# k's squares, power and product ahead of the fourth piece of the softmax; LayerNorm of tiles 0 and 1 applied in tile 3; tile 3's moments moved from two queues

## The chip, the cores and the metric

The kernel runs on one core of one Trainium2 chip. The metric is the device time of one execution in microseconds (us). The kernel before takes 2818.89 us, the median of 3 runs (2817.97 to 2821.12).

## The reference

The input is 8 sequences of 512 tokens by 256 features, float32. Three blocks follow each other: half of a transformer of two layers added to the input, a linear memory learned step by step (a scan over tokens), and the same transformer again with the same weights. Each layer of the transformer is

```
h = shift_token(x)                      # second half of the features comes from the token before
q, k, v = split(h @ wqkv)               # 8 heads of 64
q = l2norm(q) * qs;  k = l2norm(k) * ksc
q, k = rotary_xpos(q, k)
o = local_attention(q, k, v)            # windows of 128, each looks at itself and the one before
x = x + o @ wo
h = layernorm(shift_token(x)) * lg + lb
a, g = split(h @ w1 + b1);  x = x + (a * gelu(g)) @ w2 + b2
```

## The kernel before

A sequence of 512 tokens (a "batch" b, 0 to 7) is four tiles t of 128 tokens. The transformer runs twice, so there are four layers L and 32 batch-layers, each a call of `sequence(L, b, ...)` on every engine; between the two passes lies the linear memory (`mid_...`). Each engine has its own program, written out by hand in a fixed order; engines meet only in semaphores. `idx(L, b, t)` counts tiles, and `wait_ge(name, at(name, n))` waits until the n-th event of that name. There is no planner: the order of the calls in `sequence` is the order of the work.

Large products are made from a high and a low part of each operand (`split_product`, three matmuls), so ScalarE copies a product or a transpose out of a PSUM bank as the high part and VectorE subtracts that from the bank for the low part.

One tile of attention, on TensorE (`sequence`, L1223): the scores `S` (L1078) of tile t in two halves; matmuls of the down projection `W2` of the batch before as fillers (`fill`, L1219); `A1`, the q, k, v products of the tile ahead (k first); `PT`, the transposes of the softmax (L1094), four pieces of two heads each; `PV` (L1108), four pieces, the product with v; `A0`, the transposes of x two tiles ahead (L1030); `A2`, the transposes of k and q of the tile ahead (L1054); `WO`, the output projection (lines L1018 to L1020 with `oT`). After tile 2 comes `H2T(L, b, 0)` (L1133 to L1139), which transposes the normalised tiles 0 and 1. After tile 3 come `W1` for tiles 0 and 1, then `H2T(L, b, 1)` between the fifth and the sixth piece, and `W1` for tiles 2 and 3.

The softmax of tile t goes through three engines, piece by piece (j = 0 to 3): VectorE `S` (L1550) adds the mask, scales and takes the minimum; ScalarE `S` (L767) takes the exponentials of two heads and their sums; VectorE `R` (L1559) takes the reciprocals; GpSimd `NP` (L607) multiplies. TensorE's `PT j` waits for `pn_done` of piece j, ScalarE's `PT j` (L778) copies the transpose, and TensorE's `PV j` waits for that (`pt_sb`). After `PV` 3 ScalarE's `O` (L785) and VectorE's `O` (L1564) make `oT`, for which `WO` waits.

k and q of the tile ahead: ScalarE squares them (L743, L746) and copies v (L749); VectorE's `A1` sums the squares (L1518), multiplies with the two rotary tables (L1520, L1523) and adds (L1527), k first; GpSimd's `A1` bounds k's sums from below (L589), raises them to the power -1/2 (L591) and multiplies k by the result (L594), then does guard and power for q (L598, L601). TensorE's `A2` waits for k's product (`krot`) and q's sum (`qrot`). All of GpSimd's `A1` comes after the four `NP` of a tile, all of ScalarE's after the four `S`, all of VectorE's after the four `R`.

LayerNorm needs the moments of a token's own first half and of the second half of the token before. `halves` (L1583, L1584) makes the statistics of a tile, and small DMAs move them by one token. SyncE issues these in `move_stats` (L380 to L386) and `move_first_halves` (L363, L365); for tile 3 the two of `move_first_halves` are issued by ScalarE, just before its first `Gelu` (`G`). `LN_moments` joins them, GpSimd's `LN` (L624) takes the power, `LN_apply` (L1611) normalises. For tiles 0 and 1 (half 0) VectorE does all of it inside tile 2: moments between its k and q parts, applications before and after `O`. Its low part of `H2T(L, b, 0)` (L1577) stands in tile 3 between `R` 0 and `S` 3.

In the first pass, batch 4 stores the split w2 to DRAM (`store_w2`), and batch 0 of each layer splits w2 beside its second half of `W1`.

Of the kernel before, what the change touches and what calls it, by code (L numbers as in the profile page):

```python
# [39 lines left out]
P = 128  # L40
# [23 lines left out]
def build(nc, A):  # L64
    ctx = ExitStack()
    with ctx:
# [295 lines left out]
        def move_first_halves(e, t, q):  # L362
            e.dma_start(stt[0:P - 1, t + 1, 12:18], stt[1:P, t, 0:6]).then_inc(q, 16)  # L363
            if t:
                e.dma_start(stt[P - 1:P, t, 12:18], stt[0:1, t, 0:6]).then_inc(q, 16)  # L365
# [10 lines left out]
        def _(e):  # L376
            def move_stats(L, b, t, q):
# [3 lines left out]
                if t < 3:  # L381
                    move_first_halves(e, t, q)
# [131 lines left out]
            def sequence(L, b, last=False):  # L514
# [33 lines left out]
                if L < DEPTH and b == 4:  # L548
                    store_w2(L)
# [29 lines left out]
        def _(e):  # L579
            def A1(L, b, t, LN_of=None):  # L580
# [14 lines left out]
                if LN_of:  # L595
                    LN(*LN_of)
# [39 lines left out]
            def sequence(L, b, prev, nxt):  # L636
                for t in range(NT):
# [3 lines left out]
                    for j in range(4):  # L641
                        NP(L, b, t, j)
                    if ahead:
                        A1(*ahead, (L, b, 0) if t == 2 else None)
# [9 lines left out]
            def transformer(ps):  # L654

                A1(DEPTH * ps, 0, 0)
# [75 lines left out]
        def _(e):  # L732
# [6 lines left out]
            def A1(L, b, t):  # L739
# [3 lines left out]
                e.activation(sq[:, 0, :], bank[0][:, :], ACT.Square).then_inc(sqk, 1)  # L743
                e.wait_ge(q_ps, at(q_ps, m + 1))
# [103 lines left out]
            def sequence(L, b, prev, nxt):  # L848
                for t in range(NT):
                    ahead = (L, b, t + 1) if t < NT - 1 else nxt and (*nxt, 0)  # L850
                    ahead2 = (L, b, t + 2) if t < NT - 2 else nxt and (*nxt, t - 2)
                    for j in range(4):
                        S(L, b, t, j)
                    if ahead:
                        A1(*ahead)
                    for j in range(4):
                        PT(L, b, t, j)
                    O(L, b, t)
                    if ahead2:
                        A0(*ahead2)  # L860
                    if ahead:
                        A2(*ahead)
                    if t == 2:
                        H2T(L, b, 0)
# [4 lines left out]
                move_first_halves(e, 3, st_moved[1])  # L869
# [6 lines left out]
                for mt in range(MT):  # L876
                    G(L, b, 1, mt)
                    U_hi(L, b, MT + mt - 1)
                    if L < DEPTH and b == 0 and 1 <= mt <= 3:
                        split_w2_hi(L, mt - 1)  # L880
# [9 lines left out]
            def transformer(ps):  # L890
# [7 lines left out]
                A1(DEPTH * ps, 0, 0)  # L898
# [116 lines left out]
        def _(e):  # L1015
# [66 lines left out]
            def PT(L, b, t, j):  # L1082
# [7 lines left out]
                if j == 0 and t in (0, 3):  # L1090
                    e.wait_ge(h2t_lo, at(h2t_lo, 2 * b + 16 * L + (t == 3)))
# [35 lines left out]
            def H2T(L, b, half):  # L1127

                done = 9 * b + (72 * L + 4 * half)
                e.wait_ge(pt_sb, at(pt_sb, 4 * idx(L, b, 2 + half) + 4))  # L1130
# [92 lines left out]
            def sequence(L, b, prev, nxt):  # L1223
                for t in range(NT):
# [22 lines left out]
                    PV(L, b, t, 0)  # L1247
                    PT(L, b, t, 3)
                    for j in range(1, 4):
                        PV(L, b, t, j)  # L1250
# [8 lines left out]
                    if t == 2:  # L1259
                        H2T(L, b, 0)  # L1260
# [231 lines left out]
        def _(e):  # L1492
# [5 lines left out]
            def A1(L, b, t, LN_of=None):  # L1498
# [14 lines left out]
                for i, (squared, rotated, added, sums, summed, read) in enumerate((  # L1513
                        (sqk, rotk, kr_step, ssk, ssk_done, guard_k), (sqq, rotq, qrot, ssq, ssq_done, guard_q))):
                    f = 2 * (1 - i)
                    e.wait_ge(squared, at(squared, m + 1))
                    e.wait_ge(read, at(read, m))
                    e.tensor_reduce(sums[:, :], sq[:, i, :].rearrange("p (h d) -> p h d", h=HEADS), AX.X, ALU.add).then_inc(summed, 1)  # L1518
# [9 lines left out]
                    if LN_of and i == 0:  # L1528
                        LN_moments(*LN_of)
# [181 lines left out]
            def sequence(L, b, prev, nxt):  # L1711
                for t in range(NT):
# [6 lines left out]
                    if t == 3:  # L1719
                        H2T(L, b, 0)  # L1720
                    S(L, b, t, 3)
                    for j in range(1, 4):
                        R(L, b, t, j)
                        if L == 0 and b < B - 1 and j < 3:
# [6 lines left out]
                    if ahead:  # L1731
                        A1(*ahead, (L, b, 0) if t == 2 else None)
                    if L == 0 and b < B - 1 and t == 0:
                        entry_stats(b + 1, 3)
                    if t == 2:
                        LN_apply(L, b, 0, 0, 3)
                    O(L, b, t)
                    if ahead2:
                        A0(*ahead2)
# [302 lines left out]
```

## Time and profile before

| | |
|---|---|
| median of 3 runs | 2818.89 us |
| profiled execution, its own time | 2823.89 us |
| its span, first to last instruction | 2822.1 us |
| mean granted TensorE clock | 0.988 of 2.4 GHz |
| busy share: PE, DVE, ACT, POOL | 95%, 76%, 62%, 56% |
| the chain that ended last: PE, DVE, ACT, issue, POOL | 52%, 19%, 12%, 8%, 7% |

PE is TensorE's matmuls, DVE VectorE, ACT ScalarE, POOL GpSimd. L12 is line 12 of the kernel; a line can be that of a helper, so L1018 to L1020 are the matmuls of every split product, told apart by the tiles they read. The ends of matmuls are modelled, so starts are the surer times; times on POOL are rough. Everything below comes from this one execution.

### The profile page before, as it was taken

The numbers are of one execution on the slowest core, as the hardware profiler recorded it, in microseconds if no ns is written. First come the engines' busy times: TensorE is split into PE (matmuls) and PEld (weight loads), VectorE is DVE, ScalarE is ACT, GpSimd is POOL, SyncE is SP. The second block draws the span as 40 slices with busy tenths as digits, with TensorE's granted clock in tenths as the row PEclk, the third lists the DMA queues.
The fourth block names the chain that finished last, engine by engine and source line by source line (L and its number), as shares of the span: only waits on it lengthen the run. The fifth ranks groups of instructions, "written<-read, shape, count | busy, mean of one in ns | idle before, by whom it ended". The sixth has DMA issues, their size and how long they took to land.

```text
span 2822.1 us, 66713 instructions
## 1 busy us (share of the span) xinstructions
PE 2690.0 (95%) x23280; PEld 2319.4 (82%) x23280; DVE 2146.8 (76%) x6398; ACT 1757.2 (62%) x4748; POOL 1577.9 (56%) x1758
## 2 busy tenths in 40 slices
PE   7999999999999999998999999999999999999998
PEld 6888888888888888887776788888888888888887
DVE  7788888877777877776655887777777778877875
ACT  4666666666666665665454666666666666666664
POOL 4565666556555665654212566655556566656554
PEclk8999999999999999999999999999999999999999
DMA  3121011002000000004100000000003000000000
GB/s 113 31 76 58 24 51 53 20 24 104 13 2 2 2 2 24 2 2 163 58 17 31 2 2 2 2 2 2 2 2 109 32 2 17 17 17 17 17 16 24
DMA packets 75899, 81.33 MB, mean 29 GB/s; under 512 B 37552, under 2 KB 61872, under 8 KB 74416
## 3 DMA queue, kind: packets, MB, share of 16 engines
q1 hardware_dynamic: 69792, 75.51, 8.1%
q8 instruction: 189, 3.10, 0.5%
q10 hardware_dynamic: 5776, 1.56, 0.2%
q14 instruction: 142, 1.16, 0.1%
HBM read 49.53 MB, written 26.74 MB: 27 GB/s over the span
## 4 chain that ended last, share of the span: by engine, by line
PE 52%; DVE 19%; ACT 12%; issue 8%; POOL 7%; ACTq 2%; DMA 1%; DVEq 0%; POOLq 0%
PE bank L1018 9%; PE bank L1020 8%; PE bank L1019 8%; ACT pr L767 7%; PE bank L1219 5%; PE bank L1108 4%; PE bank L1078 4%; PE bank L1094 3%; PE bank L1054 3%; DVE t L1523 3%; DVE t L1520 3%; PE bank L1363 2%; POOL pr L607 2%; DVE pr L1550 2%; DVE h L1611 2%
## 5 line engine op out<-in xcount | busy, mean ns | idle before, releaser
L607 POOL TENSOR_TENSOR pr<-pr,rden 128x512 f32<-128x512 f32 (+1 forms) x512 | 467.6, 940 | 516.6 <-DVE rden L1559 512.7
L767 ACT ACTIVATE pr<-pr,nb 128x256 f32<-128x256 f32 (+1 forms) x1024 | 479.5, 470 | 276.5 <-DVE nb L1550 273.4
L1550 DVE CUSTOM_DVE_ANT_0 pr<-bank,maskb,r 128x256 f32<-128x256 f32 (+1 forms) x1024 | 401.8, 447 | 26.8 <-PE bank L1078 17.6
L1018 PE MATMUL bank<-h2T,w 128*128 128x256 f32 x1408 | 406.8, 289 | 12.9 <-DVE h2T L1577 12.9
L1019 PE MATMUL bank<-h2T,w 128*128 128x256 f32 x1408 | 395.9, 281 | 0.0
L1020 PE MATMUL bank<-h2T,w 128*128 128x256 f32 x1408 | 395.7, 281 | 0.0
L634 POOL TENSOR_TENSOR uTl<-t,uTh 128x256 fp32r<-128x256 f32 x320 | 238.1, 748 | 277.3 <-ACT uTh L842 277.3
L1625 DVE SCALAR_TENSOR_TENSOR t<-bank,b,t 128x256 f32<-128x256 f32 (+1 forms) x384 | 181.8, 480 | 215.5 <-ACT t L830 102.2
L1018 PE MATMUL bank<-wqkv,hT 128*128 128x512 f32 x768 | 306.2, 399 | 8.5 <-DVE nb L1550 5.7
L1019 PE MATMUL bank<-wqkv,hT 128*128 128x512 f32 x768 | 305.5, 398 | 0.0
L1020 PE MATMUL bank<-wqkv,hT 128*128 128x512 f32 x768 | 302.5, 394 | 0.0
L778 ACT ACTIVATE pT<-bank 128x512 f32<-128x512 f32 (+1 forms) x512 | 250.9, 550 | 68.0 <-PE bank L1094 67.9
L1018 PEld LDWEIGHTS bank<-h2T,w 128*128 128x128 f32 x1408 | 268.0, 190 | 22.9 <-DVE h2T L1577 19.0
L1019 PEld LDWEIGHTS bank<-h2T,w 128*128 128x128 f32 x1408 | 270.7, 192 | 0.0
L1108 PE MATMUL bank<-pT,v 128*64 128x128 f32 x3584 | 263.9, 283 | 6.2 <-ACT pT L778 1.9
L1020 PEld LDWEIGHTS bank<-h2T,w 128*128 128x128 f32 x1408 | 265.7, 189 | 0.0
L1094 PE MATMUL bank<-ident,pr 128*128 128x128 f32 x1792 | 249.1, 279 | 6.2 <-POOL pr L607 6.2
L1108 PEld LDWEIGHTS bank<-pT,v 128*64 128x64 f32 x3584 | 201.2, 137 | 55.8 <-issue 51.9
L827 ACT ACTIVATE t<-bank,b 128x256 f32<-128x256 f32 x320 | 151.5, 474 | 149.6 <-PE bank L1020 145.2
L1094 PEld LDWEIGHTS bank<-ident,pr 128*128 128x128 f32 x1792 | 202.9, 142 | 47.4 <-issue 22.4
L1219 PE MATMUL bank<-w2h,uTh 128*128 128x256 f32 (+1 forms) x768 | 237.7, 310 | 2.9 <-issue 1.5
L1078 PE MATMUL bank<-kT,qT 64*128 64x256 f32 (+1 forms) x3072 | 232.9, 286 | 3.8 <-issue 2.9
(229 smaller groups left out, 6978.3 us busy)
## 6 DMA issues: line engine op xcount, KB each, us to landing
wqkv<-wqkv_split SPq DMA_DIRECT2D x18, 512.0 KB, 6.2
w<-w_split SPq DMA_DIRECT2D x3, 2816.0 KB, 9.9
Y<-in_x SPq DMA_DIRECT2D x8, 512.0 KB, 8.2
out<-Y SPq DMA_DIRECT2D x8, 512.0 KB, 3.5
stt<-stt SPq DMA_DIRECT2D x224, 3.0 KB
h<-out SPq DMA_DIRECT2D x7, 512.0 KB, 3.9
out<-h SPq DMA_DIRECT2D x7, 512.0 KB, 2.9
wqkv_split<-wqkv SPq DMA_DIRECT2D x1, 3072.0 KB, 11.7
```

Source lines behind the costliest of these rows:

```text
L607: e.tensor_tensor(pr[:, 2 * j:2 * j + 2, 0:wide], pr[:, 2 * j:2 * j + 2, 0:wide], rden[:, 2 * j:2 * j + 2].unsqueeze(2).to_broadcast([P, 2 ...
L634: e.tensor_tensor(uTl[:, half, JOBS[i], :], ut[:, job % 2, :], uTh[:, half, JOBS[i], :], ALU.subtract).then_inc(u_lo, 1)
L767: last = e.activation(pr[:, hd, 0:wide], pr[:, hd, 0:wide], ACT.Exp, bias=nb[:, hd:hd + 1], scale=-1.0, accum_out=den[:, hd:hd + 1])
L778: e.activation(pT[:, 2 * j:2 * j + 2, 0:w, :], bank[PT_BANK[j]][:, :].rearrange("p (h w c) -> p h w c", h=2, w=2)[:, :, 0:w, :], ACT.Copy) ...
L1018: e.matmul(out, left[0], right[0], start=first, stop=False)
L1019: e.matmul(out, left[0], right[1], start=False, stop=False)
L1020: return e.matmul(out, left[1], right[0], start=False, stop=last)
L1078: m = e.matmul(out, qT[rows, lq, p, :], kT[rows, lk, p, slots, :], start=(i == 0), stop=(i == 2), skip_group_check=True)
L1094: mm = e.transpose(bank[bk][:, (2 * g + w) * P:(2 * g + w + 1) * P], pr[:, 2 * j + g, w * P:(w + 1) * P], ident[:, :])
L1108: mm = e.matmul(bank[6][64 * g:64 * g + 64, j * P:(j + 1) * P], v[:, tile, hd * DH:(hd + 1) * DH], pT[:, hd, w, :], start=(w == 0), stop=( ...
L1219: mm = e.matmul(bank[bk][:, 0:D], left, right, start=(unit == 0), stop=(unit == UNITS - 1))
L1550: m = e.tensor_tensor_reduce(pr[:, hd, 0:wide], bank[j][:, g * 256:g * 256 + wide], far, r[:, t, 1, place(hd):place(hd) + 1], FAR, ALU.add ...
```

## The change

In each tile that has a tile ahead, three engines do k's part earlier. ScalarE squares k before its fourth pair of exponentials; VectorE sums k's squares before its fourth reciprocal (`squares` is the old code as a function); GpSimd does guard, power and product of k before the fourth `NP`. On TensorE `PV` 1 and 2 go ahead of `PT` 3. LayerNorm's moments of tiles 0 and 1 are joined after the second reciprocal of tile 2, GpSimd's `LN` goes behind q's power, and the four applications go between the reciprocals of tile 3; `H2T(L, b, 0)` goes behind `PV` 3 of tile 3 on all three engines. Of tile 3's three statistics moves SyncE issues two and ScalarE one row only (before: SyncE one, ScalarE two). `U_rest` goes ahead of `LN_moments` in the first half of `W1`. `store_w2` waits for the statistics to have moved, and w2 is split one piece of `W1` earlier.

```diff
-        def move_first_halves(e, t, q):
-            e.dma_start(stt[0:P - 1, t + 1, 12:18], stt[1:P, t, 0:6]).then_inc(q, 16)
-            if t:
-                e.dma_start(stt[P - 1:P, t, 12:18], stt[0:1, t, 0:6]).then_inc(q, 16)
+        def move_first_row(e, t, q):
+            e.dma_start(stt[P - 1:P, t, 12:18], stt[0:1, t, 0:6]).then_inc(q, 16)
...
                 e.wait_ge(st_done, at(st_done, idx(L, b, t) + 1))
                 e.dma_start(stt[1:P, t, 6:12], stt[0:P - 1, t + 1, 18:24]).then_inc(q, 16)
-                if t < 3:
-                    move_first_halves(e, t, q)
+                e.dma_start(stt[0:P - 1, t + 1, 12:18], stt[1:P, t, 0:6]).then_inc(q, 16)
+                if 0 < t < 3:
+                    move_first_row(e, t, q)
...
                 if L < DEPTH and b == 4:
+                    stats_moved(L, b)
                     store_w2(L)
...
@@ -638,10 +640,15 @@
                     ahead = (L, b, t + 1) if t < NT - 1 else nxt and (*nxt, 0)
                     if prev:
                         XB(*prev, t)
-                    for j in range(4):
+                    for j in range(3):
                         NP(L, b, t, j)
                     if ahead:
-                        A1(*ahead, (L, b, 0) if t == 2 else None)
+                        A1_k(*ahead)
+                    NP(L, b, t, 3)
+                    if ahead:
+                        A1_q(*ahead)
+                    if t == 2:
+                        LN(L, b, 0)
...
                 for t in range(NT):
                     ahead = (L, b, t + 1) if t < NT - 1 else nxt and (*nxt, 0)
                     ahead2 = (L, b, t + 2) if t < NT - 2 else nxt and (*nxt, t - 2)
-                    for j in range(4):
+                    for j in range(3):
                         S(L, b, t, j)
                     if ahead:
-                        A1(*ahead)
+                        A1_k(*ahead)
+                    S(L, b, t, 3)
+                    if ahead:
+                        A1_qv(*ahead)
                     for j in range(4):
                         PT(L, b, t, j)
                     O(L, b, t)
+                    if t == 3:
+                        H2T(L, b, 0)
                     if ahead2:
                         A0(*ahead2)
                     if ahead:
                         A2(*ahead)
-                    if t == 2:
-                        H2T(L, b, 0)
                 for i in next_pieces(L, b)[0:1]:
                     next_hi(i)
                 table(ACT.Gelu)
                 e.wait_ge(st_done, at(st_done, idx(L, b, 3) + 1))
-                move_first_halves(e, 3, st_moved[1])
+                move_first_row(e, 3, st_moved[1])
...
                 for mt in range(MT):
                     G(L, b, 1, mt)
                     U_hi(L, b, MT + mt - 1)
-                    if L < DEPTH and b == 0 and 1 <= mt <= 3:
-                        split_w2_hi(L, mt - 1)
+                    if L < DEPTH and b == 0 and mt < 3:
+                        split_w2_hi(L, mt)
...
@@ -1087,8 +1102,8 @@
                     e.wait_ge(nb_done, at(nb_done, 4 * n + 4))
                 else:
                     e.wait_ge(pt_sb, at(pt_sb, 4 * n + (0, -2, 0, 1)[j]))
-                if j == 0 and t in (0, 3):
-                    e.wait_ge(h2t_lo, at(h2t_lo, 2 * b + 16 * L + (t == 3)))
+                if j == 0 and t == 0:
+                    e.wait_ge(h2t_lo, at(h2t_lo, 2 * b + 16 * L))
...
-                e.wait_ge(pt_sb, at(pt_sb, 4 * idx(L, b, 2 + half) + 4))
+                e.wait_ge(pt_sb, at(pt_sb, 4 * idx(L, b, 3) + 4))
...
                     PT(L, b, t, 1)
                     PT(L, b, t, 2)
                     fill(1)
-                    PV(L, b, t, 0)
+                    for j in range(3):
+                        PV(L, b, t, j)
                     PT(L, b, t, 3)
-                    for j in range(1, 4):
-                        PV(L, b, t, j)
+                    PV(L, b, t, 3)
+                    if t == 3:
+                        H2T(L, b, 0)
                     if ahead2:
                         A0(*ahead2)
                     if ahead:
@@ -1256,8 +1273,6 @@
                     if ahead:
                         A2(*ahead, 1)
                     WO(L, b, t)
-                    if t == 2:
-                        H2T(L, b, 0)
                     fill(3)
...
+                for i, (rotated, added) in enumerate(((rotk, kr_step), (rotq, qrot))):
                     f = 2 * (1 - i)
-                    e.wait_ge(squared, at(squared, m + 1))
-                    e.wait_ge(read, at(read, m))
-                    e.tensor_reduce(sums[:, :], sq[:, i, :].rearrange("p (h d) -> p h d", h=HEADS), AX.X, ALU.add).then_inc(summed, 1)
+                    if i:
+                        squares(m, 1)
...
-                    if LN_of and i == 0:
-                        LN_moments(*LN_of)
+
+            def squares(m, i):
+
+                squared, sums, summed, read = ((sqk, ssk, ssk_done, guard_k), (sqq, ssq, ssq_done, guard_q))[i]
+                e.wait_ge(squared, at(squared, m + 1))
+                e.wait_ge(read, at(read, m))
+                e.tensor_reduce(sums[:, :], sq[:, i, :].rearrange("p (h d) -> p h d", h=HEADS), AX.X, ALU.add).then_inc(summed, 1)
...
                     S(L, b, t, 1)
                     S(L, b, t, 2)
                     R(L, b, t, 0)
-                    if t == 3:
-                        H2T(L, b, 0)
                     S(L, b, t, 3)
                     for j in range(1, 4):
+                        if j == 3 and ahead:
+                            squares(idx(*ahead), 0)
                         R(L, b, t, j)
+                        if t == 2 and j == 1:
+                            LN_moments(L, b, 0)
+                        if t == 3 and j < 3:
+                            LN_apply(L, b, 0, 2 * j - 2, 2 * j)
                         if L == 0 and b < B - 1 and j < 3:
...
                     if ahead:
-                        A1(*ahead, (L, b, 0) if t == 2 else None)
+                        A1(*ahead)
                     if L == 0 and b < B - 1 and t == 0:
                         entry_stats(b + 1, 3)
-                    if t == 2:
-                        LN_apply(L, b, 0, 0, 3)
                     O(L, b, t)
+                    if t == 3:
+                        H2T(L, b, 0)
                     if ahead2:
                         A0(*ahead2)
-                    if t == 2:
-                        LN_apply(L, b, 0, 3)
                     if ahead:
                         A2(*ahead)
                     WO(L, b, t)
...
                 for mt in range(MT):
                     U(L, b, 0, mt)
                     if mt == 1:
+                        U_rest(L, b, 0)
                         LN_moments(L, b, 1)
-                        U_rest(L, b, 0)
                     if mt == 2:
...
@@ -1762,8 +1782,8 @@
                     U(L, b, 1, mt)
                     if mt == 1:
                         U_rest(L, b, 1)
-                    if L < DEPTH and b == 0 and mt > 2:
-                        split_w2_lo(L, mt - 3)
+                    if L < DEPTH and b == 0 and 2 <= mt <= 4:
+                        split_w2_lo(L, mt - 2)
```

## Rows read from the trace of the kernel before

**Rows 1.** The page, part 1: busy us (share of the span) xinstructions.

```profile
PE 2690.0 (95%) x23280; PEld 2319.4 (82%) x23280; DVE 2146.8 (76%) x6398; ACT 1757.2 (62%) x4748; POOL 1577.9 (56%) x1758
```

**Rows 2.** Who TensorE waited for, whole run: us in total, times, longest.

```profile
PE bank L1018 <- DVE oT L1564: 32.4, 40, 1.0
...
PE bank L1135 <- DVE h L1611: 11.8, 25, 3.8
```

**Rows 3.** Timeline of GpSimd, tile 1: start, us, operation, count, [idle before <-releaser].

```profile
2271.43 4.04 POOL L607 TENSOR_TENSOR pr<-pr,rden 128x512 f32<-128x512 f32 x4 [5.01 <-DVE rden L1559]
2275.43 0.24 POOL L589 TENSOR_SCALAR ssg<-ssk 128x8 f32<-128x8 f32 x1
2275.76 1.66 POOL L591 TENSOR_TENSOR r<-ssg,small 128x8 f32<-128x8 f32 x1
2277.57 1.04 POOL L594 TENSOR_TENSOR t<-t,r 128x512 f32<-128x512 f32 x1
```

**Rows 4.** Timeline of ScalarE, tile 1.

```profile
2272.65 0.49 ACT L767 ACTIVATE pr<-pr,nb 128x256 f32<-128x256 f32 x1
...
2273.64 0.58 ACT L743 ACTIVATE sq<-bank 128x512 f32<-128x512 f32 x1
...
2277.52 0.60 ACT L778 ACTIVATE pT<-bank 128x512 f32<-128x512 f32 x1 [0.46 <-PE bank L1094]
```

**Rows 5.** Timeline of VectorE, tile 1.

```profile
2273.77 0.17 DVE L1559 RECIPROCAL rden<-den 128x2 f32<-128x2 f32 x1 [0.82 <-ACT pr L767]
...
2274.25 0.69 DVE L1518 TENSOR_REDUCE ssk<-sq 128x8 f32<-128x512 f32 x1 [0.31 <-ACT sq L743]
```

**Rows 6.** Timeline of TensorE, tile 1.

```profile
2276.23 0.66 PE L1108 MATMUL bank<-pT,v 128*64 128x128 f32 x8
2276.82 0.66 PE L1094 MATMUL bank<-ident,pr 128*128 128x128 f32 x4
2277.41 1.58 PE L1108 MATMUL bank<-pT,v 128*64 128x128 f32 x24
2278.92 0.44 PE L1030 MATMUL bank<-ident,Y 128*128 128x128 f32 x2
...
2280.50 0.36 PE L1018 MATMUL bank<-wo,oT 128*128 128x256 f32 x1
```

**Rows 7.** Timeline of GpSimd, tile 0.

```profile
2260.59 0.24 POOL L589 TENSOR_SCALAR ssg<-ssk 128x8 f32<-128x8 f32 x1 [0.56 <-DVE ssk L1518]
```

**Rows 8.** Timeline of TensorE, tile 0.

```profile
2263.34 0.44 PE L1030 MATMUL bank<-ident,Y 128*128 128x128 f32 x2
...
2265.69 0.36 PE L1018 MATMUL bank<-wo,oT 128*128 128x256 f32 x1
```

**Rows 9.** Timeline of TensorE, tile 2.

```profile
2293.72 0.44 PE L1030 MATMUL bank<-ident,Y 128*128 128x128 f32 x2
...
2296.31 0.36 PE L1018 MATMUL bank<-wo,oT 128*128 128x256 f32 x1 [0.88 <-DVE oT L1564]
```

**Rows 10.** Timeline of GpSimd, tile 3.

```profile
2302.60 1.04 POOL L607 TENSOR_TENSOR pr<-pr,rden 128x512 f32<-128x512 f32 x1 [5.26 <-DVE rden L1559]
2304.13 3.04 POOL L607 TENSOR_TENSOR pr<-pr,rden 128x512 f32<-128x512 f32 x3 [0.49 <-DVE rden L1559]
```

**Rows 11.** Timeline of TensorE, tile 3.

```profile
2309.88 0.44 PE L1030 MATMUL bank<-ident,Y 128*128 128x128 f32 x2
```

**Rows 12.** Stretches: length and busy us (x) of PE, PEld, DVE, ACT, POOL; PEclk; DMA.

```profile
756.00:759.30 3.30, 1.90 (x21) 1.58 (x19) 3.30 (x9) 2.61 (x6) 1.46 (x2) 1.00 0.00 0
759.40:766.20 6.80, 6.80 (x29) 5.80 (x29) 2.40 (x17) 3.87 (x17) 3.76 (x6) 0.50 0.01 2
2295.40:2298.80 3.40, 2.52 (x23) 2.39 (x23) 3.36 (x9) 0.83 (x3) 1.94 (x2) 1.00 0.00 0
745.10:828.00 82.90, 79.49 (x636) 69.51 (x636) 63.52 (x187) 52.71 (x144) 47.24 (x53) 0.96 0.02 5
828.00:907.20 79.20, 76.77 (x636) 66.99 (x636) 60.78 (x184) 50.98 (x141) 47.20 (x53) 1.00 0.01 2
```

More of the change, by code:

```diff
@@ L579, in _, with A1_k @@
         def _(e):
-            def A1(L, b, t, LN_of=None):
+            def A1_k(L, b, t):
                 m = idx(L, b, t)
@@ L594, in A1, with A1_q @@
                 e.tensor_tensor(heads(kr), heads(kr), r[:, t, 0, :].unsqueeze(2).to_broadcast([P, HEADS, DH]), ALU.mult).then_inc(krot, 1)
-                if LN_of:
-                    LN(*LN_of)
+            def A1_q(L, b, t):
+                m = idx(L, b, t)
+                minus_half = small[:, 0:1].to_broadcast([P, HEADS])
                 e.wait_ge(ssq_done, at(ssq_done, m + 1))
@@ L654, in transformer @@
             def transformer(ps):
-                A1(DEPTH * ps, 0, 0)
+                A1_k(DEPTH * ps, 0, 0)
+                A1_q(DEPTH * ps, 0, 0)
                 if ps == 0:
@@ L737, in A0, with A1_k @@
                 e.activation(columns(hT, 0, t * P, P), cut(bank[2][:, 0:D], KT), ACT.Copy).then_inc(ht_hi, 1)
-            def A1(L, b, t):
+            def A1_k(L, b, t):
                 m = idx(L, b, t)
@@ L743, in A1, with A1_qv @@
                 e.activation(sq[:, 0, :], bank[0][:, :], ACT.Square).then_inc(sqk, 1)
+            def A1_qv(L, b, t):
+                m = idx(L, b, t)
                 e.wait_ge(q_ps, at(q_ps, m + 1))
@@ L897, in transformer @@
                     split_hi(2)
-                A1(DEPTH * ps, 0, 0)
+                A1_k(DEPTH * ps, 0, 0)
+                A1_qv(DEPTH * ps, 0, 0)
                 A0(DEPTH * ps, 0, 1)
@@ L1496, in A0, with A1 @@
                 e.tensor_tensor(columns(hT, 1, t * P, P), cut(bank[2][:, 0:D], KT), columns(hT, 0, t * P, P), ALU.subtract).then_inc(ht_lo, 1)
-            def A1(L, b, t, LN_of=None):
+            def A1(L, b, t):
                 m = idx(L, b, t)
@@ L1511, in heads @@
                     return ap.rearrange("p (h c j) -> p h c j", h=HEADS, c=2)
-                for i, (squared, rotated, added, sums, summed, read) in enumerate((
-                        (sqk, rotk, kr_step, ssk, ssk_done, guard_k), (sqq, rotq, qrot, ssq, ssq_done, guard_q))):
+                for i, (rotated, added) in enumerate(((rotk, kr_step), (rotq, qrot))):
                     f = 2 * (1 - i)
-                    e.wait_ge(squared, at(squared, m + 1))
-                    e.wait_ge(read, at(read, m))
-                    e.tensor_reduce(sums[:, :], sq[:, i, :].rearrange("p (h d) -> p h d", h=HEADS), AX.X, ALU.add).then_inc(summed, 1)
+                    if i:
+                        squares(m, 1)
                     e.wait_ge((kt_ps, qt_ps)[i], at((kt_ps, qt_ps)[i], m))
@@ L1803, in transformer @@
                     e.tensor_copy(maskb[:, :, :, :].rearrange("p a w k -> p (a w k)"), mask_raw)
+                squares(idx(DEPTH * ps, 0, 0), 0)
                 A1(DEPTH * ps, 0, 0)
```

## The prediction

> **What bounds the kernel now.** I read the page's first part, then who waited for whom on TensorE, then one batch in order of time, engine by engine, and last the granted clock. The first part says that TensorE is busy 95% of the span [rows 1]: whatever the other engines do counts only where TensorE stands still. The table of waits says where: 32.4 us in the output projection for VectorE's `oT`, 11.8 us in front of the transposes of tiles 2 and 3 for LayerNorm's `h` [rows 2]. So the present waits are worth a few tens of us in 2819, and the question is what new ones the change makes. I work it on batch 1 of the last layer (its tiles lie between 2254 and 2314 us), whose pattern repeats in 32 batch-layers of about 79 us.
>
> **The moved k part on GpSimd, tile 1.** In time order GpSimd normalises four pieces of the softmax (`NP`) one after the other, 4.04 us from 2271.43, and only then does k's guard, power and product: 2275.43, 2275.76, 2277.57 to 2278.61, so 3.14 us from the first start to when the next can start [rows 3]. The change puts these 3.14 us ahead of piece 3. Are k's sums there in time? ScalarE squares k now at 2273.64, after the fourth pair of exponentials; that pair starts at 2272.65 [rows 4], so the new Square starts there and the pair behind it (its input is k's product, the first of three that TensorE makes meanwhile). VectorE's reduce follows a Square by 0.61 (2274.25 after 2273.64) and takes 0.69 [rows 4, 5]: done at 2273.95, before GpSimd has finished piece 2 at 2274.46. The fourth pair's exponentials slip by 0.48 us, VectorE's last reciprocal from 2273.77 to 2274.25, and the rotation of k still starts a little earlier than now; its sum is ready before the power ends. So nothing holds the k part up, and nothing shortens it: piece 3 ends at 2274.46 + 3.14 + 1.04 = 2278.6 instead of 2275.5.
>
> **What TensorE does about it.** It transposes piece 3 (`PT 3`) now at 2276.82, 1.3 us after the piece is ready; PV 1 to 3 start at 2277.41 and the next step, A0, at 2278.92 [rows 6]. The new order puts PV 1 and 2 ahead of PT 3. PV 0 with its change-over takes 0.59, three more take 1.51, so PV 0 to 2 are over at 2276.23 + 0.59 + 1.01 = 2277.8. Piece 3 comes at 2278.7 with a semaphore's delay: TensorE stands 0.9 us. Then the second price of the new order: ScalarE's copy of PT 3 starts 0.70 after it (2277.52 after 2276.82) and takes 0.60 [rows 4, 6]; with 0.1 for the release PV 3 starts 1.4 after PT 3. Before, PV 1 and 2 lay in between; now nothing does, and 0.6 of the 1.4 is PT 3 itself: another 0.8. A0 starts at 2278.7 + 1.4 + 0.5 = 2280.6, 1.7 us late. Behind PV 3 everything follows PV 3: the copy and difference of `oT` set the output projection (`WO`) 1.58 us after A0 [rows 6], as now. Tile 1 costs **+1.7 us**. The first wait is bounded by 0 (GpSimd not late at all) and 1.9 (TensorE profits nothing from PV 1 and 2), the second by 0 and 1.4.
>
> **Tile 0.** Its pieces are half as wide. The power cannot start before the sums, and k's guard now starts at 2260.59, after a wait for them [rows 7]; with the Square one pair earlier I take 0.9 less, so the k part runs 2259.7 to 2262.8 and piece 3 to 2263.4. The same two waits put A0 1.5 late. But between A0 and WO there are now 2.35 us instead of tile 1's 1.58 [rows 8], waits for k's and q's rotation, and these 0.8 vanish, since VectorE is ahead. **+0.7** (bounds -0.8 and 1.7).
>
> **Tile 2.** A0 at 1.7 late as in tile 1. WO comes 2.59 after A0 because VectorE still has the moments and four applications of LayerNorm to do before `oT`; TensorE waits 0.88 for it there [rows 9]. The change takes both away (moments to the wait for exponentials after the second reciprocal, applications to tile 3), so WO is 1.58 after A0 again: 1.7 - 1.0 = **+0.7** (bounds -1.0 and 1.7). The moments need tile 1's moved statistics some 4.6 us earlier than now; if these are late, the wait falls first on VectorE's own wait for exponentials, so I take 0 (bounds 0 and 0.5 a batch). GpSimd's `rs` now stands behind q's power, where it is idle.
>
> **Tile 3.** Now VectorE puts `h2T` between reciprocal 0 and the fourth pair, and GpSimd starts piece 1 only at 2304.13 [rows 10]. With `h2T` gone pieces 0 to 2 run from 2302.60 to 2305.7; four applications lie between the reciprocals, 0.3 us each, where VectorE waited for exponentials. Piece 3 ends at 2305.7 + 3.14 + 1.04 = 2309.8; PT 3 would be reached at 2308.6. Wait 1.2, then 0.8. A0 now is at 2309.88 [rows 11]; it comes 1.9 late. One wait behind it (0.2, k's product) goes; but H2T (0.7 us of TensorE) leaves tile 2, where it lay between WO and the scores, and VectorE is not ready for the scores that much sooner: 0.2 back. **+1.9**, in 30 of 32 cases, since after the last batch of each pass no tile is ahead. H2T itself only moves, and ScalarE's and VectorE's copies of it lie under A0, A2, WO and the last fill before W1 needs them.
>
> **The rest.** Tile 3's moments: SyncE now issues two of the moves and ScalarE one, so gelu starts up to 0.7 us earlier and LayerNorm's second half some tenths earlier. That recovers at most the 11.8 us of waits for `h`, among them one of 3.8 which falls where `store_w2` is issued, which now stands behind a wait [rows 2]; I take 11 (bounds 0 and 12). w2's split one step earlier: the batch that has it takes 82.9 us instead of 79.2 [rows 12], twice in the run: 7.4 (bounds 0 and 7.4). Both together give **-18**.
>
> The Trainium skill, page "DMA: Bandwidth & Descriptors", section "Issuing engines are not separate DMA queues", says that DMAs of several engines run on the same 16 DMA engines, and that starting them from two saves only the sequencer's time. By that rule alone the ordinary `h` waits (8 of my 11 us) would stay, and the sum would be 3010. I go by the row, since ScalarE's issue time is what gelu waits behind.
>
> **The clock.** In the stretch 756.0 to 759.3, with a stall in it, TensorE was busy 1.90 of 3.30 us at full clock, and from 759.4 to 766.2 it was granted 0.50, which is 1.2 GHz; around tile 2's present stall, 2295.4 to 2298.8, it was busy 2.52 of 3.40 and kept 2.4 GHz [rows 12]. The new stages have about 1.7 us (tiles 1 and 2) or 2.0 us (tile 3) of stall within 3 us, so they are like the first stretch or worse, and how they fall varies from stage to stage. Most of the 3.7 us by which that batch is longer is stall 1.4 and clock 2.3. I take one fall in four stages (a third of tiles 1 and 2, half of tile 3, few of tile 0: 35 falls) at 1.3 us, as part of a fall lies under waits: **+45** (bounds 0 and 128 falls of 2.3, 294).
>
> **Sum.** 32 x (0.7 + 1.7 + 0.7) = 99, and 30 x 1.9 = 57: 156. Less 18, plus 45: +183. The profiled execution took 2823.89 us for a span of 2822.1, 5 us above the median 2818.89; the differences are taken from it and put on the median: **3002 us**.
>
> **Rivals.**
> *The clock stays up.* The stalls come as worked out, but full clock is kept, as through today's 0.88: 2819 + 156 - 18 = 2957. For it: the stalls lie between transposes and products, never one long gap. Against: 756.0. Chance 0.22.
> *The clock falls in most stages.* 96 falls at 1.5: 2957 + 144 = 3101. Chance 0.15.
> *Only the second wait.* If piece 3 is there by the end of PV 2, tile 1 costs 0.8, tile 0 -0.2, tile 2 -0.2, tile 3 +0.8: 32 x 0.4 + 30 x 0.8 - 18 = +19, 2838. It needs 0.9 us less on GpSimd; spans on it are rough, but that is more than a quarter of the k part [rows 3]. Chance 0.03.
> *The other side, faster.* The place is PT 3. If GpSimd's k part took under 1.5 us instead of 3.14, piece 3 and its copy would lie wholly under PV 1 and 2, and the stalls of today would be the whole effect: 32.4 and 11.8 [rows 2], 0.8 in 32 tiles 0 [rows 8], 7.4 [rows 12], together 77: 2742. Nothing in the trace shows a power of less than 1.6 us. Chance 0.04. That it lands within 0.2%: 0.02.
>
> **How the numbers follow.** My case has 0.54; its own range is 2960 to 3050. The range for 8 in 10 leaves the faster cases and the extreme clock out: 2915 to 3085. A measurement of this kernel tells 0.2% (6 us) from no change; faster 0.04, same 0.02, slower 0.94.
>
> **What would show it.** In the trace after: TensorE waits in PT (L1094's form) for GpSimd's product with `rden` some 0.9 us in each tile, 126 times, and in PV for ScalarE's copy of pT as often, 0.8 us; the wait of WO for `oT` in tile 2 is gone; H2T follows PV 3 of tile 3; the wait for `h` is near nothing; a batch takes 84 us or more; the clock shows 0.5 in many short stretches, all behind PT 3. Wrong it is if piece 3's product does not start after k's, if TensorE reaches PT 3 later than 2 us after PV 0, or if the granted clock stays near 0.99.

## The result: 9.8% slower, and the profile after

| | before | after |
|---|---|---|
| median | 2818.43 us (2816.38 to 2821.12) | 3093.81 us (3089.06 to 3103.08) |
| ratio | | 1.098, 95% interval 1.0951 to 1.101 |
| profiled execution: time, span | 2823.89, 2822.1 us | 3097.28, 3095.5 us |
| mean granted TensorE clock | 0.988 | 0.958 |
| stretches granted 0.5, in all | 12, 68.0 us | 55, 263.7 us |

Slower, as forecast, but by 275 us and not by 183. The page's first part, the chain that ended last, and who TensorE waited for (us in total, times, longest):

```profile
PE 2761.2 (89%) x23280; PEld 2396.3 (77%) x23280; DVE 2254.7 (73%) x6398; ACT 1752.1 (57%) x4748; POOL 1592.7 (51%) x1758
...
PE 43%; POOL 21%; DVE 16%; issue 11%; ACT 8%; DMA 0%; DVEq 0%; ACTq 0%; SPq 0%; POOLq 0%
```

```profile
PE bank L1109 <- POOL pr L609: 182.8, 130, 2.7
PE bank L1123 <- ACT pT L789: 82.4, 132, 0.7
...
PE bank L1150 <- DVE h L1629: 2.9, 8, 1.2
```

TensorE's share falls from 95% to 89% [rows 1], and GpSimd has 21% of the chain where it had 7%. L1109 is `PT`, L1123 `PV`, L1150 the first transpose of `h`. The wait for `oT` (32.4 us in 40 places, rows 2) is gone from the head of the table, that for `h` at the first transpose fell from 11.8 to 2.9, and two waits stand in nearly every tile that were next to nothing. Tile 1 of a batch, GpSimd and then TensorE, answers to rows 3 and 6:

```profile
2843.89 3.04 POOL L609 TENSOR_TENSOR pr<-pr,rden 128x512 f32<-128x512 f32 x3 [5.55 <-DVE rden L1577]
2846.90 0.24 POOL L589 TENSOR_SCALAR ssg<-ssk 128x8 f32<-128x8 f32 x1
2847.22 1.67 POOL L591 TENSOR_TENSOR r<-ssg,small 128x8 f32<-128x8 f32 x1
2849.03 1.04 POOL L594 TENSOR_TENSOR t<-t,r 128x512 f32<-128x512 f32 x1
2850.03 1.04 POOL L609 TENSOR_TENSOR pr<-pr,rden 128x512 f32<-128x512 f32 x1
```

```profile
2848.69 1.55 PE L1123 MATMUL bank<-pT,v 128*64 128x128 f32 x24
2851.13 0.66 PE L1109 MATMUL bank<-ident,pr 128*128 128x128 f32 x4 [0.89 <-POOL pr L609]
2852.47 0.67 PE L1123 MATMUL bank<-pT,v 128*64 128x128 f32 x8 [0.69 <-ACT pT L789]
2853.07 0.44 PE L1045 MATMUL bank<-ident,Y 128*128 128x128 f32 x2
```

Piece 3 starts 3.13 us after the guard starts (3.14 worked out), TensorE waits 0.89 for it (0.9) and 0.69 for the copy (0.8). From VectorE's first score of tile 1 to that of tile 2 it is 16.50 us, where before it was 14.81: +1.69 against +1.7. The same distance of tile 0 went from 14.39 to 15.03: +0.64 against +0.7.

Tile 3 is where it parts. VectorE, GpSimd and TensorE there, in this order:

```profile
2792.38 0.16 DVE L1577 RECIPROCAL rden<-den 128x2 f32<-128x2 f32 x1
2792.45 0.35 DVE L1624 TENSOR_TENSOR lead<-mv,rs 128x2 f32<-128x2 f32 x1
2792.73 1.40 DVE L1629 TENSOR_SCALAR h<-Y,mv,rs 128x128 f32<-128x128 f32 x2
2794.05 0.15 DVE L1577 RECIPROCAL rden<-den 128x2 f32<-128x2 f32 x1
2794.12 1.30 DVE L1629 TENSOR_SCALAR h<-Y,mv,rs 128x128 f32<-128x128 f32 x2
2795.35 0.67 DVE L1547 TENSOR_REDUCE ssk<-sq 128x8 f32<-128x512 f32 x1
```

```profile
2791.75 2.04 POOL L609 TENSOR_TENSOR pr<-pr,rden 128x512 f32<-128x512 f32 x2 [5.26 <-DVE rden L1577]
2794.28 1.06 POOL L609 TENSOR_TENSOR pr<-pr,rden 128x512 f32<-128x512 f32 x1 [0.49 <-DVE rden L1577]
2796.11 0.24 POOL L589 TENSOR_SCALAR ssg<-ssk 128x8 f32<-128x8 f32 x1 [0.77 <-DVE ssk L1547]
```

```profile
2800.33 0.66 PE L1109 MATMUL bank<-ident,pr 128*128 128x128 f32 x4 [2.58 <-POOL pr L609]
2801.67 0.67 PE L1123 MATMUL bank<-pT,v 128*64 128x128 f32 x8 [0.69 <-ACT pT L789]
```

Two applications that I put at 0.3 us each take 1.40 and 1.30 together. Each pair ends only after GpSimd's product beside it has: 2794.13 against 2793.79, 2795.42 against 2795.34. In all 32 batches one of the two takes 1.14 us in the first pair and 1.06 in the second, and the other 0.32 to 0.34. Reciprocal 2 and the sum of k's squares come later for it, so GpSimd stands 0.49 and 0.77, and TensorE waits 2.58 where I had 1.2. In tile 2 the same is seen on a smaller scale, with LayerNorm's moments in their new place (`vare` is the variance, made by a `TENSOR_SCALAR` too); VectorE, then TensorE:

```profile
2776.17 0.92 DVE L1617 TENSOR_SCALAR vare<-mv 128x4 f32<-128x4 f32 x1
2777.01 0.15 DVE L1577 RECIPROCAL rden<-den 128x2 f32<-128x2 f32 x1
```

```profile
2782.48 0.66 PE L1109 MATMUL bank<-ident,pr 128*128 128x128 f32 x4 [1.10 <-POOL pr L609]
```

The Trainium skill, page "SBUF — State Buffer", section "Who interferes with whom", says that VectorE and GpSimd share a pair of ports as an exclusive lock, that `tensor_scalar` is among VectorE's operations that can take the pair, and that whoever issues first holds it for the whole instruction. The trace agrees: `h` is made by `TENSOR_SCALAR`, and its pair is stretched from 0.6 to 1.40 us beside a product of 1.04 us. The application that was already running when the product began kept its 0.32. That it is the ports which VectorE waits for is the page's account; the runs below show only that these instructions are slow beside GpSimd's products and others are not.

Two whole batches of after, one without a stretch of low clock and one with three (length; busy us of PE, PEld, DVE, ACT, POOL; PEclk; DMA):

```profile
2716.90:2802.30 85.40, 76.41 (x638) 66.91 (x636) 66.35 (x187) 50.53 (x140) 47.90 (x53) 1.00 0.05 14
2450.80:2540.20 89.40, 80.39 (x638) 70.60 (x636) 64.35 (x183) 50.84 (x140) 48.07 (x53) 0.94 0.08 25
```

At full clock a batch is 6.2 us longer than the 79.2 of rows 12: 32 x 6.2 = 198 us. The rest, about 77 of the 275, goes with the clock. Of the 55 stretches at 0.5, 23 begin in tile 3, 15 in tile 2, 5 in tile 1 and 7 in tile 0, most of them behind `PT` 3; before there were 2, 1, 0 and 3.

### The profile page after: what moved, and what is told of

Read it like the earlier page. It is cut to its first block, busy times and chain, and to the rows that moved or that the text cites. A ratio compares the mean times of both kernels' runs of the same rounds, so it can differ in the third digit from the quotient of the medians.

```text
span 3095.5 us, 66726 instructions
## 1 busy us (share of the span) xinstructions
PE 2761.2 (89%) x23280; PEld 2396.3 (77%) x23280; DVE 2254.7 (73%) x6398; ACT 1752.1 (57%) x4748; POOL 1592.7 (51%) x1758
## 4 chain that ended last, share of the span: by engine, by line
PE 43%; POOL 21%; DVE 16%; issue 11%; ACT 8%; DMA 0%; DVEq 0%; ACTq 0%; SPq 0%; POOLq 0%
POOL pr L609 10%; PE bank L1033 6%; PE bank L1035 6%; PE bank L1034 5%; POOL r L591 5%; PE bank L1069 5%; PE bank L1234 5%; DVE pr L1568 4%; PE bank L1123 3%; PE bank L1109 3%; DVE h L1629 2%; ACT pT L789 2%; ACT pr L778 2%; PE bank L1378 2%; PE bank L1045 2%
## 5 line engine op out<-in xcount | busy, mean ns | idle before, releaser
L1109 PE MATMUL bank<-ident,pr 128*128 128x128 f32 x1792 | 255.2, 283 | 182.9 <-POOL pr L609 182.8
L1109 PEld LDWEIGHTS bank<-ident,pr 128*128 128x128 f32 x1792 | 206.2, 144 | 233.3 <-POOL pr L609 215.5
L1123 PE MATMUL bank<-pT,v 128*64 128x128 f32 x3584 | 270.6, 292 | 84.0 <-ACT pT L789 82.4
L1123 PEld LDWEIGHTS bank<-pT,v 128*64 128x64 f32 x3584 | 204.7, 141 | 142.0 <-ACT pT L789 114.3
L1582 DVE TENSOR_TENSOR oT<-bank,oT 128x512 fp32r<-128x512 f32 x128 | 88.5, 692 | 281.0 <-ACT oT L796 281.0
L626 POOL TENSOR_TENSOR rs<-vare,small 128x4 f32<-128x4 f32 x64 | 69.7, 1088 | 342.4 <-DVE vare L1617 342.4
```

The lines of the kernel that those rows point to most:

```text
L1109: mm = e.transpose(bank[bk][:, (2 * g + w) * P:(2 * g + w + 1) * P], pr[:, 2 * j + g, w * P:(w + 1) * P], ident[:, :])
L1123: mm = e.matmul(bank[6][64 * g:64 * g + 64, j * P:(j + 1) * P], v[:, tile, hd * DH:(hd + 1) * DH], pT[:, hd, w, :], start=(w == 0), stop=( ...
```

## The experiments

The changes below are against the kernel after, unless they say before. "Kernel 3" is the kernel of experiment 3, and so on; of two kernels under one number it is the first. The runs of before that stood beside them had medians of 2817 to 2822 us.

**1. The parts alone.** Three kernels from the kernel before, each with one part of the diff shown ahead: the k part with TensorE's order; LayerNorm's place (with `H2T`); the rest (moments, `store_w2`, w2's split).

> The k part of the change alone (ScalarE's Square, VectorE's sums, GpSimd's guard, power and product ahead of the fourth piece; PV 1 and 2 ahead of PT 3); LayerNorm, the statistics moves and w2's split as before. Theory A (two new waits on TensorE in every tile, 1.7 us in tile 1): most of the 275 us comes from here, 2819 + 155 for the waits + 40 to 80 for the granted clock, 3010 to 3055. Rival B (LayerNorm's applications in tile 3, which took 1.40 and 1.30 us for two instead of 0.6 in the trace after, are what my sum missed and the greater part): under 2960.

> LayerNorm's part alone (moments after the second reciprocal of tile 2, applications between the reciprocals of tile 3, H2T behind PV 3 of tile 3). Theory A: it takes 1.0 us of WO's wait out of tile 2 and puts up to 1.5 us of VectorE into tile 3, of which the transposes of k wait for about 1: 2800 to 2840. Rival B: 2870 or more.

> The rest alone (tile 3's moves from two queues, U_rest ahead of the moments, store_w2 behind a wait, w2 split one step earlier). As predicted -18: 2801; if the two-queue move brings nothing and only the two single stalls go, -8 to -11: 2809.

| part | median, us | ratio, 95% interval | against before |
|---|---|---|---|
| k part | 3034.95 | 1.0754 (1.0729 to 1.0779) | +213 |
| LayerNorm | 2797.16 | 0.9921 (0.9907 to 0.9936) | -24 |
| the rest | 2809.72 | 0.9961 (0.9946 to 0.9976) | -12 |
| sum of the three | | | +177 |
| all together | 3093.81 | 1.098 (1.0951 to 1.101) | +275 |

The k part came out as expected (3010 to 3055), the rest as in its second case (2809), and the LayerNorm part 3 us below its range. The two other parts are gains by themselves, and together with the k part they cost 98 us more than the sum. Some of that was never to be had: with the k part alone the wait for `oT` is nearly gone already (before 32.4), since `PV` 3 comes later there, and LayerNorm's new place can't take it away a second time:

```profile
PE bank L1033 <- DVE oT L1584: 3.1, 6, 1.0
```
In the LayerNorm part the applications are as slow as in the change:

```profile
2282.81 1.40 DVE L1609 TENSOR_SCALAR h<-Y,mv,rs 128x128 f32<-128x128 f32 x2
2284.20 1.30 DVE L1609 TENSOR_SCALAR h<-Y,mv,rs 128x128 f32<-128x128 f32 x2
```

There they cost TensorE nothing at `PT` 3 (it waits 6.1 us there in all, before 6.2), since piece 3 has slack. With the k part ahead of piece 3 that slack is spent. In the rest alone, the wait for `h` went from 11.8 us to

```profile
PE bank L1135 <- DVE h L1611: 5.8, 27, 1.2
```

so the one wait of 3.8 is gone and the ordinary ones mostly stay; that is 6 of the 11 us I had counted. The Trainium skill, page "DMA: Bandwidth & Descriptors", section "Issuing engines are not separate DMA queues", says that issuing from several engines saves only the issuing time on the sequencer, by which I had the ordinary ones stay. Of 8.0 us of them 5.8 did, nearer to that than to my reading of the row. But this is no test of it: two engines issued tile 3's moves before as well (SyncE one, ScalarE two), and the part has other edits with it.

**2. TensorE's old order.** `PV` 0, `PT` 3, `PV` 1 to 3 again:

```diff
-                    for j in range(3):
-                        PV(L, b, t, j)
+                    PV(L, b, t, 0)
                     PT(L, b, t, 3)
-                    PV(L, b, t, 3)
+                    for j in range(1, 4):
+                        PV(L, b, t, j)
```

> The changed kernel with TensorE's old order (PT 3 right behind PV 0, then PV 1 to 3). Theory A: TensorE comes to PT 3 1.0 us earlier and waits 1.9 instead of 0.9, but PV 1 and 2 lie under ScalarE's copy, so the second wait of 0.8 goes: within 20 us of the changed kernel, 3075 to 3110. Rival (the new order of TensorE is itself what costs, the second wait of 0.8 in 126 tiles is avoidable): 100 us less, 2990.

3127.5 us (3125.72 to 3130.31), 34 more than after; ratio to before 1.109 (1.1073 to 1.1106). The wait of `PV` goes and that of `PT` grows by 98.4 us:

```profile
PE bank L1109 <- POOL pr L609: 281.2, 131, 3.5
```

That is 18 us above my range. The waits make 98.4 - 82.4 = 16 of the 34; the clock is at 0.5 for 287.2 us instead of 263.7. Given that piece 3 is late, the new order is the better one. What it costs once piece 3 is in time is another question (kernels 7 and 8).

**3. The applications behind the rotations of tile 3.**

```diff
-                        if t == 3 and j < 3:
-                            LN_apply(L, b, 0, 2 * j - 2, 2 * j)
...
                         A1(*ahead)
...
+                    if t == 3:
+                        LN_apply(L, b, 0)
                     O(L, b, t)
```

> The changed kernel with the four applications of tile 3 behind k's and q's rotations instead of between the reciprocals. Theory A (between the reciprocals VectorE's tensor_scalar waits for GpSimd's running product: two took 1.40 us instead of 0.6, so k's sums and piece 2 come late and TensorE's wait before PT 3 of tile 3 is 2.6 us instead of 1.2): that wait falls by 1.4 in 30 tiles, with the clock's share 40 to 70 us less, 3025 to 3055. Rival (the 98 us by which the parts together cost more than one by one are clock falls that any stall brings): under 20 us less, 3075 or more.

3008.84 us (3002.55 to 3020.43): 85 less than after. The applications are back to a mean of 425 ns over the whole kernel (before 422, after 591), and TensorE's wait for piece 3 fell by 40.3 us:

```profile
PE bank L1109 <- POOL pr L609: 142.5, 129, 2.2
```

That is 30 x 1.34, what tile 3 had over my 1.2. The 85 are more than the 40 to 70 expected. The other 45 us are left for the clock, which is at 0.5 for 118.5 us here instead of 263.7: at full clock tiles 0 to 2 are as long as in the kernel after. Half of these 145 us would be 73, so part of the low clock there lay under waits.

**4. Other instructions of VectorE in the same places.** Kernel 3 with two `bn_stats` of 128x128 in each of the two places where the applications had been:

```diff
+                        if t == 3 and j < 3:
+                            for i in range(2):
+                                e.bn_stats(...)
```

> As the run with late applications, with two statistics instructions of the same size (128 columns of x, about 0.29 us each, results not used) in each of the two places between the reciprocals of tile 3. If it is the wait for GpSimd that costs there, these cost nothing beside it, since VectorE waits for exponentials: within 10 us of that run. If it is the instructions' own time, back to within 15 us of the changed kernel, 3080 or more.

3012.36 us (3006.15 to 3015.05), the same as kernel 3. The stand-ins take their own time beside the same products:

```profile
L1746 DVE BATCH_NORM_STATS2 stt<-Y 128x6 f32<-128x128 f32 x128 | 29.8, 275 | 0.0
```

So 0.28 us each in those places is indeed free (TensorE's wait for piece 3 is 141.2 us), as I had said of the applications; what was wrong was their length beside GpSimd.

**5. Idle matmuls in the two waits.** Of a 128x128 identity into a free bank, 3 to 10 ahead of `PT` 3 and 2 or 3 ahead of `PV` 3. They add work to TensorE; what it waits for comes no earlier by them.

> The changed kernel with idle matmuls of the identity (float32, result never read) in the two waits of TensorE: 3 before PT 3 (10 in tile 3) and 2 or 3 before PV 3, about as long as the waits, so that TensorE is busy there and the chain is not lengthened. Theory A: the granted clock rises from 0.958 to 0.98 or more, and what the clock cost comes back: 60 to 90 us less, 3005 to 3035. Rival (the clock costs little, since its falls lie under waits; the waits themselves are the 275 us): less than 25 us less, 3070 or more.

3014.71 us (3012.74 to 3017.42), 79 less than after, ratio to before 1.069 (1.0675 to 1.0706); mean granted clock 0.992, at 0.5 for 48.7 us. From VectorE's first scores of a batch's tile to those of the next tile, the four tiles take 15.1, 16.5, 16.7 and 37.1 us at full clock (medians; the last with the MLP) both here and after, so with the idle matmuls no tile is shorter or longer but by the clock. So of the 275 us some 79 are the clock's.

**6. The power shortened.** GpSimd's power of k's sums replaced by a product (k is scaled wrongly): 0.20 us instead of 1.67.

```diff
-ssg[:, 0, :], minus_half, ALU.pow).then_inc(rk_done, 1)
+ssg[:, 0, :], minus_half, ALU.mult).then_inc(rk_done, 1)
```

> The changed kernel with GpSimd's power for k's norm replaced by a product (about 0.25 us instead of 1.67), so k is scaled wrongly; the order is the same. Theory A: the k part takes 1.7 us instead of 3.1, piece 3 is there about when PV 2 ends: the first wait nearly goes (0.9 in tiles 0 to 2, 1.4 of 2.6 in tile 3), 128 us, and with it most of the clock's share: 2890 to 2945. Rival (what holds piece 3 is the wait for k's sums, not the power): less than 50 us less, 3045 or more.

3058.11 us (3052.25 to 3063.29): only 36 less than after, a miss. The number is the rival's, but not its reason: GpSimd's guard does not wait for k's sums in tile 1. GpSimd in tile 1 shows why:

```profile
2809.78 0.24 POOL L589 TENSOR_SCALAR ssg<-ssk 128x8 f32<-128x8 f32 x1
2810.11 0.20 POOL L591 TENSOR_TENSOR r<-ssg,small 128x8 f32<-128x8 f32 x1
2811.75 1.05 POOL L594 TENSOR_TENSOR t<-t,r 128x512 f32<-128x512 f32 x1 [1.44 <-DVE t L1540]
2812.75 1.04 POOL L609 TENSOR_TENSOR pr<-pr,rden 128x512 f32<-128x512 f32 x1
```

k's product now stands 1.44 us for VectorE's addition of the rotated k (182.8 us in 128 tiles), which in the kernel after ends just inside the power:

```profile
2848.10 0.69 DVE L1540 TENSOR_TENSOR t<-t 128x512 f32<-128x512 f32 x1
```

It ends at 2848.79, the power at 2848.89. Two things that end together hold the product, and piece 3 is queued behind both. The run said where to cut: the product itself.

**7. The product behind piece 3.** Kernel 3 with k's product in a function of its own; guard and power stay ahead of piece 3.

```diff
                         A1_k(*ahead)
                     NP(L, b, t, 3)
                     if ahead:
+                        A1_product(*ahead)
                         A1_q(*ahead)
```

> The change with the four applications of tile 3 moved behind q's and k's rotations (as in apply_late, 3009 us, waits of TensorE 142.5 us for the softmax's fourth piece and 83.0 us for the copy of pT) and GpSimd's product of k put behind piece 3; guard and power stay ahead of it. In the run with the short power, the product waited 1.43 us each for VectorE's addition, which is why the power's 1.46 us bought nothing. Theory (what holds piece 3 back is the whole k part, product included, and the product cannot start before VectorE's addition): piece 3 starts 1.04 us earlier in every tile, the wait of TensorE for it falls to 10 to 50 us, the wait for the copy of pT stays near 83 us, and the time is 2860 to 2920 us. Rival (only the power and the sums count, as I took when I shortened the power): the product's place is worth no more than 40 us, time above 2965. Rival (k's product late holds up A2 and so the next tile's S): waits for the products appear in its place, time above 2940.

2839.26 us (2836.45 to 2842.11), ratio to before 1.0077 (1.0062 to 1.0092): 170 less than kernel 3 by the place of one instruction of 1.04 us, and 21 below my range. Who TensorE waited for:

```profile
PE bank L1131 <- ACT pT L797: 83.0, 134, 0.7
...
PE bank L1117 <- POOL pr L615: 9.5, 17, 2.1
```

133 us of waits are gone, and the clock is at 0.5 for 32.2 us instead of 118.5; half of these 86 is 43, and 133 + 43 = 176, near the 170. No wait for the products appears. With the short power as well:

> product_behind with GpSimd's power of k's sums replaced by a product (0.21 instead of 1.67 us; k is scaled wrongly, all else is computed). Now nothing else of k stands ahead of piece 3, so the power's price must show. Theory: the wait for piece 3 goes to under 10 us, the wait for the copy of pT (0.6 us in each tile, from the new order of TensorE) stays near 83 us and alone keeps the kernel above LayerNorm part plus rest: 2840 to 2890 us, 10 to 40 us below product_behind. Rival (the order costs nothing once the piece is in time, the copy of pT is then hidden): 2780 to 2800 us.

2835.12 us (2834.02 to 2835.3), 4 less, where I had expected 10 to 40 (2840 to 2890). The wait for piece 3 is 4.8 us there, so the power ahead of it costs hardly anything once the product is out of the way: `PV` 0 to 2 cover it.

**8. The change without its k part, and another place for the applications.**

> The change without its k part: k's squares, power and product and TensorE's order as before, LayerNorm of tiles 0 and 1 applied in tile 3, moments of tile 3 from two queues, w2's split a step earlier. LayerNorm part alone gave -24 us, the rest alone -12 us against the same kernel before (2821.6). Theory (the two parts touch different waits, the oT wait of 32 us and the h waits at the start of the MLP): their sum, 2785 us, 2778 to 2793. Rival (the moments' way is hidden already by LayerNorm's new place, or both shorten the same wait): no better than the LayerNorm part, 2794 to 2800.

2776.93 us (2774.25 to 2777.81), ratio to before 0.9854 (0.9839 to 0.9869): 40 us faster than before, the fastest of all, and 4 more than the sum of its parts. Against kernel 7, 62 us lower: the wait of `PV` for the copy of pT, 83.0 us there, is not in its table. Kernel 7 differs from it in k's place and in that of the applications too, and kernel 7 with TensorE's old order was not tried, so what the new order alone costs once piece 3 is in time stays open.

The second one is the rest alone with the moments as in the change and all four applications behind `O` and `A0` of tile 2:

```diff
-                    if t == 2:
-                        LN_apply(L, b, 0, 0, 3)
                     O(L, b, t)
                     if ahead2:
                         A0(*ahead2)
                     if t == 2:
-                        LN_apply(L, b, 0, 3)
+                        LN_apply(L, b, 0)
```

> The rest alone, with LayerNorm's moments of tiles 0 and 1 taken between the reciprocals of tile 2 and all four applications behind the additions to oT of tile 2 instead of ahead of them (before) or in tile 3 (the change). TensorE waited 32.4 us in 32 stages for oT behind three applications. Theory (only their place ahead of oT costs; they need not go to tile 3): the oT wait falls under 3 us, and since VectorE's applications are then not next to GpSimd's product they take 0.3 to 0.45 us each, and h is ready for H2T as before: 2775 to 2795 us, as fast as ln_rest or faster. Rival (they hold A0 and A2 of VectorE up in turn, so that k and q of tile 3 come later): a wait at the scores of tile 3 of 0.5 us or more in 30 stages, 2800 to 2820 us.

2784.16 us (2781.83 to 2784.89), ratio to before 0.988 (0.9865 to 0.9894). The wait for `oT` fell from 32.9 us in the rest alone to

```profile
PE bank L1018 <- DVE oT L1562: 5.3, 9, 1.0
```

where I had expected under 3. Each measured against the runs of before beside it, this kernel gains 33 us and the rest alone 12: 21 us more, near the 24 that the LayerNorm part gained alone. So most of that gain needs no move to tile 3, only that no application stands ahead of `O` in tile 2; the moments moved as well, and the run does not separate the two. The applications take 422 ns each here and 586 in the fastest kernel, which still is 7 us ahead: beside GpSimd they are slower, and with slack at piece 3 TensorE hardly waits for it (6.1 us before `PT` 3 there).

## Why the prediction failed, step by step

- *Tiles 0 and 1*: right. The k part was not held up and not shortened, the two waits are near the sizes worked out, and the tiles are +0.64 and +1.69 us. "Its sum is ready before the power ends" is right too, but by 0.10 us only, which I had not worked out and which spoiled kernel 6.
- *Tile 2*: the wait for `oT` went, as said. That the moments would cost nothing between the reciprocals is not quite so: `vare`, a `TENSOR_SCALAR` again, takes up to 922 ns there instead of 172 at most. Before `PT` 3 of tile 2 TensorE waits 39.2 us in 32 batches, and 29.9 with the k part alone, where the moments are in their old place: 9 us in all, at full clock 1.10 instead of 0.89 a batch, for which I had 0.
- *Tile 3*: the step that failed. "Four applications lie between the reciprocals, 0.3 us each, where VectorE waited for exponentials": they took 1.40 and 1.30 a pair, for a wait of 2.58 and not 1.2. Kernel 3 measures 40 us of waits for it; kernel 4 shows that it is neither the order nor the 0.3 us. The trace before had the sign:

```profile
L1611 DVE TENSOR_SCALAR h<-Y,mv,rs x288: 333/341/807, 76.7 to 2799.0; 128x128 f32<-128x128 f32 x144
```

  These are minimum, median and maximum in ns. The long ones, about 60 of 0.70 to 0.81 us, lie beside GpSimd's product `uTl` (128x256); beside its power they take 0.34. The whole batch closes with it: my four tiles sum to 5.0 us, less 0.3 for `h`, plus 1.4 and 0.2 for tile 2's moments gives 6.3, and 6.2 was measured at full clock.
- *The clock*: mechanism right, size wrong, the second term that failed. I took 35 falls at 1.3 us, 45 us; there were 43 more stretches at 0.5 than before, 196 us more in all, and kernel 5 measures 79 us. At 79 / 43 = 1.8 us each, both the count and the price were low. I had half of tile 3's and a third of tile 1's and 2's stages; it was 23 of tile 3's 32, 15 of tile 2's and 5 of tile 1's. Part of it is tile 3's longer stall: kernel 3 gives 45 us back beside its waits.
- *The rest*: -18 foretold, -12 measured alone.
- The two terms, +41 for tile 3 and +34 for the clock, with 9 for tile 2 and 6 for the rest, make 90 of the 92 us by which I was low. Each is known to a few us only, so the close sum is partly luck.
- *Rivals*: "only the second wait" is what kernel 7 built, and its 2839 us is the 2838 worked out for it, though with the applications in another place; by tiles at full clock it is -0.3, +0.7, -0.9 and +1.2 us where I had -0.2, +0.8, -0.2 and +0.8, so the match to 1 us is partly luck (`H2T`, 0.7 us, has moved from tile 2 to tile 3). "The clock stays up" at 2957 would have been further off. "In most stages", 3101, is the nearest number, but not for its reason: the clock fell 43 times more, not 96.

## What to carry to other kernels

What an engine is made to do ahead of a shared step has to be weighed against that step's reader, and the last instruction of the group is the one to move back: here a product of 1.04 us, needed by nobody soon, cost 170 us in 3009. A gap in an engine's timeline is worth its length only to operations that don't need what its neighbour is using: look in the trace for the same operation beside the neighbour's work before taking its duration from elsewhere. And parts of a change that are gains alone can be losses together when both draw on the same slack or end the same wait, so measure each by itself.

## What was not expected of the hardware

A `TENSOR_SCALAR` of 128x128 on VectorE takes 0.33 us by itself; beside a GpSimd product of 1.04 us a pair took 1.30 to 1.40 and a single one 1.15 at most; one of 128x4 goes from 0.17 to 0.92. Beside GpSimd's power, in the kernel before, the 128x128 one took 0.34. `BATCH_NORM_STATS2` of 128x128 in the same place keeps its 0.28. And taking no wait away but filling it with idle matmuls gave back 79 us of 3094, with the mean granted clock up from 0.958 to 0.992.
